# Three interleaved streams on one core: PSUM banks handed out in the order of the steps, and a new order of the steps

## The reference

```python
x = hidden                                                   # [4, 1024, 128]
x = layernorm(x + global_then_local_attention(x))            # 16 heads of 8, 4 key/value heads
x = layernorm(x + top2_of_8_experts(x))                      # 128 -> 512 -> 128, gelu
x = layernorm(x + linear_attention(x))                       # one head of 64, causal
for l in range(2):                                           # 8 heads of 64, windows of 64 tokens
    q, k, v = split(shift(x) @ wqkv[l])
    q, k = rotary(l2norm(q) * qs[l]), rotary(l2norm(k) * ks[l])
    x = x + local_attention(q, k, v) @ wo[l]
    h = layer_norm(shift(x)) @ w1[l] + b1[l]
    x = x + (a * gelu(g)) @ w2[l] + b2[l]                    # a, g = split(h)
x = layernorm(x_before_the_loop + x)
```

## Time and profile before

| | |
|---|---|
| median of three runs | 2167.21 us |
| the profiled execution, its own time | 2185.86 us |
| span of its records | 2184.1 us |
| mean granted TensorE clock | 0.861 of full |
| PE busy | 1683.2 us, 77% |
| PE weight loads | 1086.1 us, 50% |
| ACT busy | 1242.6 us, 57% |
| DVE busy | 1102.8 us, 50% |
| POOL busy | 778.1 us, 36% |
| mean DMA rate | 50 GB/s |

### The profile page before, as it was taken

How to read it: one execution, slowest core, us unless ns; L and a number is a source line. 1 busy time by engine, 2 the same in 40 slices (tenths; PEclk the granted TensorE clock), 3 DMA queues, 4 the chain that set the end, 5 groups by cost and what they waited for, 6 DMA issues and landing times.

```text
span 2184.1 us, 37425 instructions
## 1 busy us (share of the span) xinstructions
PE 1683.2 (77%) x13911; PEld 1086.1 (50%) x13911; DVE 1102.8 (50%) x2039; ACT 1242.6 (57%) x2819; POOL 778.1 (36%) x654
## 2 busy tenths in 40 slices
PE   4875477767559999869559999789689887778786
PEld 2124324434535765457334766467357555546454
DVE  4114601035586434584685334684863458475563
ACT  3663256843148989655147999553367565265462
POOL 2430161150159234720167233810471353062450
PEclk7787568976669999988779999978899999899898
DMA  4000023310121232100021233100223420010010
GB/s 144 1 1 1 0 78 98 112 41 1 46 77 48 76 95 89 46 8 1 20 80 45 76 92 93 46 9 1 63 69 90 127 75 23 5 45 21 25 28 10
DMA packets 64214, 109.52 MB, mean 50 GB/s; under 512 B 12464, under 2 KB 37284, under 8 KB 63908
## 3 DMA queue, kind: packets, MB, share of 16 engines
q1 hardware_dynamic: 58339, 98.23, 15.4%
q0 software_dynamic: 4096, 8.40, 1.3%
q10 hardware_dynamic: 1600, 0.52, 0.1%
HBM read 74.40 MB, written 15.93 MB: 41 GB/s over the span
## 4 chain that ended last, share of the span: by engine, by line
PE 42%; DVE 23%; ACT 14%; POOL 9%; issue 8%; DMA 2%; another core or an unknown queue 1%; SPq 1%; ACTq 0%; DVEq 0%; POOLq 0%
PE PH L826 5%; PE PD L1050 4%; PE PB L1151 3%; PE PB L1218 3%; ACT back_arena L1525 3%; POOL front_arena L2229 3%; PE PB L1238 3%; ACT front_arena L1360 2%; PE PD L874 2%; POOL fy L2297 2%; PE PB L1172 2%; ACT middle_arena L1473 2%; PE PD L1061 2%; PE PB L1274 2%; DVE back_arena L2085 2%
## 5 line engine op out<-in xcount | busy, mean ns | idle before, releaser
L1360 ACT ACTIVATE front_arena<-PD 128x1024 f32<-128x1024 f32 (+3 forms) x384 | 294.4, 815 | 96.5 <-PE PD L874 87.7
L2229 POOL TENSOR_TENSOR front_arena<-front_arena,tri 128x256 f32<-128x256 f32 x256 | 193.0, 771 | 338.5 <-ACT front_arena L1360 337.3
L2292 POOL TENSOR_TENSOR back_arena<-back_arena 128x512 f32<-128x512 f32 x128 | 182.7, 1434 | 270.2 <-DVE back_arena L2088 269.5
L1218 PE MATMUL PB<-wqkv,hT 128*128 128x512 f32 x384 | 226.7, 682 | 38.2 <-DVE back_arena L2088 13.3
L1525 ACT ACTIVATE back_arena<-PB,fnm 128x128 f32<-128x128 f32 x512 | 181.3, 373 | 85.8 <-DVE fnm L2095 85.5
L826 PE MATMUL PH<-front_arena 128*32 128x512 f32 (+3 forms) x1536 | 193.2, 575 | 37.5 <-POOL front_arena L2229 33.9
L2297 POOL TENSOR_TENSOR fy<-fm,minus_half 128x16 f32<-128x16 f32 x64 | 191.6, 2993 | 56.6 <-DVE fm L2111 54.7
L2282 POOL TENSOR_TENSOR bs_y<-bs_m,minus_half 128x4 f32<-128x4 f32 x24 | 24.3, 1011 | 400.0 <-DVE bs_m L2017 400.0
L2095 DVE TENSOR_REDUCE fnm<-PB 128x4 f32<-128x512 f32 x128 | 88.3, 690 | 153.3 <-PE PB L1238 135.6
L874 PE MATMUL PD<-front_arena 32*128 32x512 f16 (+3 forms) x768 | 128.9, 369 | 46.9 <-ACT middle_arena L1473 18.7
L1238 PE MATMUL PB<-back_arena 64*64 64x128 f32 x2048 | 145.0, 283 | 0.0
(11 more groups left out here) (294 smaller groups left out, 3553.9 us busy)
## 6 DMA issues: line engine op xcount, KB each, us to landing
W<-in_W SPq DMA_DIRECT2D x48, 514.0 KB
middle_arena<-in_W SPq DMA_DIRECT2D x44, 514.0 KB
back_arena<-back_arena SPq DMA_DIRECT2D x128, 128.0 KB
xpos<-x_tables SPq DMA_DIRECT2D x64, 128.0 KB
y_rows<-middle_arena SPq DMA_DIRECT2D x20, 256.0 KB, 5.4
middle_arena<-x_rows SPq DMA_DIRECT2D x8, 512.0 KB, 4.7
x_tables<-back_arena SPq DMA_DIRECT2D x1, 2048.0 KB, 7.5
out_y<-Nb SPq DMA_DIRECT2D x64, 32.0 KB, 1.6
```

Source lines behind the costliest of these rows:

```text
L1218: pe.matmul(p, hT[:, 128 * i:128 * i + 128], wqkv[:, l, c:c + 512], start=True, stop=True).then_inc(filled(b, "f" + n, l, i), 1)
L1360: act.activation(pb[:, :, 0:n], p[:, :, 0:n], ACT.Exp, scale=INV_SQRT_HD).then_inc(freed(b, "S", half, g, kc, jp), 1)
L2229: pool.tensor_tensor(pb, pb, tri[:, :].unsqueeze(1).to_broadcast([128, 2, 128]), ALU.mult).then_inc(sg("masked"), 1)
L2292: pool.tensor_tensor(T1[k % 2][:, hs, :], T1[k % 2][:, hs, :], T2[:, hs, :], ALU.add).then_inc(sg("rot"), 1)
```

## The change

Two things are changed together. First the places in PSUM: all eight banks are one tensor, a slot is (kind, first bank), and each step in turn is given that slot, of those it may use, whose banks were given out longest ago; it waits for the former users of all banks that the slot covers. Until the first step of a back, front and middle have three double slots (banks 0, 2 and 6) and the sums two single ones (4 and 5). From then on it is as before: double slots at 0 and 2, sums at 4, the back at 5, 6 and 7. Once the last global attention is done the back has bank 4 too, and after the last step that needs a double slot it has all eight.

Second, the table RUNS is another one. The number and kinds of the steps, what each does, and the order within each stream are the same.

```diff
 class Tickets:
-        self.size = {"D": 2, "H": 1, "B": 3}
-    def add(self, kind, *key):
-        k = self.next[kind] % self.size[kind]
+    def add(self, slots, *key):
+        def banks(slot):
+            return range(slot[1], slot[1] + (2 if slot[0] == "D" else 1))
+        def oldest(slot):
+            return max(self.stamp[k] for k in banks(slot))
+        slot = min(slots, key=oldest)
+        former = sorted({self.last[k] for k in banks(slot)} - {None})
...
+PAIRED = [("D", 0), ("D", 2)]
+SUMS = [("S", 4)]
+LATE = [("S", 5), ("S", 6), ("S", 7)]
...
-F153 M1 F4 M2 F6 M1 F2 M1 F2 M1 F2 M2 F1 M2 F4 M1 F2 M1 F4 M1 F4 M1 F4 M1
+F156 M2 F1 M1 F1 M2 F1 M4 F2 M1 F2 M1 F2 M1 F4 M5 F1 M1 F2 M1 F1 M2 F2 M3
...
+            if kind == "D":
+                t.add(PAIRED if begun else PAIRED + [("D", 6)], b, *(("gate",) if n == "gate" else label))
+            elif kind == "H":
+                t.add(SUMS if begun else SUMS + [("S", 5)], b, "O", rest[0], rest[1])
+            else:
+                slots = LATE + (SUMS if summed else []) + ([("S", k) for k in range(4)] if left["D"] == 0 else [])
...
         def fill(pe, *key):
-            kind, k, n = tk.at[key]
-            if n:
+            for (kind, k), n in tk.at[key][2]:
                 pe.wait_ge(sg(f"free_{kind}{k}"), n)
...
                     pe.wait_ge(sg("weights2"), 16 * len(second))
+                    fill(pe, "w_b1")
```

153 lines of the change are left out of this document (76 added, 77 removed).

## The result

The changed kernel takes 2067.58 us (median of 4 runs, 2057.81 to 2076.29), the kernel before 2165.92 in the same session (4 runs, 2161.36 to 2169.61). The ratio is 0.9546 with a 95% interval of 0.9497 to 0.9595: 98 us faster. I had predicted 2137 us, range 2100 to 2188.

What follows compares the result with a forecast made beforehand. No engine bounds the kernel; the order of the work does, by how well it fills PE. Terms 231 + 275 + 1077 + 300 + 271 = 2154 against a 2184 us span, 30 less, giving 2137 us, range 2100 to 2188.

Steps and rivals of the forecast that it cites:

- the fill: F1 with M0: the pieces of M0's chain sum to 275 us against 353, so B0 starts 78 us earlier.
- Experts under 115 us: Sign in F1 with M0: the prediction is wrong if M0's experts take over 115 us.
- Twelve pairs at 8.4 us: M0's experts within F1: twelve pairs take 100 us, against 126.3 before.
- the bound of 72: M0's experts: 72 us for twelve pairs if bound by the weights alone, with two pairs in flight.
- 933 us: From B0's start to M3's start: PE work of 933 us, which with 144 idle makes 1077.
- The sign that I had named for the opposite: Starts of F2 and F3: wrong if stretches with busy DVE and idle PE return with their full 27 us.
- the term of 300: M3 with the rest of B2: M3's chain pieces sum to 302, taken as 300 us, against 355 before.
- The chain bounds this stretch, not PE: M3 with the rest of B2: M3's dependent chain sets the time, with PE idle for 104 us.
- No PE row is in it, so in those tiles a free bank gains nothing: B3's tiles: the 10.29 us cycle has no PE row, so eight banks gain 3 us, bounds 0 and 24.
- Rival 1: B3, M3's stretch and F0: banks decide more, 43 us beyond the forecast, 2094 us; chance 0.20.
- Rival 2: M0 and M3: the experts' chain doesn't get shorter, price 74 us, 2211 us, or 2186 with two thirds; chance 0.13.
- Rival 3: Middle of the kernel: idle just moves, every round still loses 80 us, 1118 for 1077, 2178 us; chance 0.14.

Runs made afterwards that it cites:

- The loads in two parts: Changed kernel, with the first product's columns of each expert's weights loaded one product earlier, the rest as before: 2035.62 us, ratio 0.9377.
- without the early ones: Changed kernel without the third double slot (D6) and second sums bank (S5) ahead of the first back: 2102.0 us, ratio 0.9699.
- The late round alone: Kernel before with the new banks and old order through F3, M2, B1; then 92 steps of B2 alone, then M3 with B2's rest as changed: 2165.59 us.
- the second product first: Changed kernel, with the second product of expert pair i - 1 ahead of the first product of pair i: 2159.39 us, ratio 0.9946.
- thin weights: Changed kernel, but after the first four expert loads each fetches only 64 of 1028 columns: 2037.0 us, ratio 0.9400.
- the banks alone: Kernel before with the changed kernel's bank rule and the old table RUNS: 2150.91 us, ratio 0.9907.

## Why the prediction was wrong

By its terms, in us of the profiled span:

| stretch | predicted | measured | of which PE idle, predicted / measured |
|---|---|---|---|
| F0 | 231 | 231 | - / 90 |
| F1 with M0 | 275 | 275 | - / 80 |
| 506 to M3's start | 1077 | 1046 | 144 / 139 |
| M3 with the rest of B2 | 300 | 259 | 104 / 55 |
| B3 | 271 | 263 | - / 51 |
| sum | 2154 | 2074 | |

These are 80 us of span. The medians (2137 and 2067.6) differ by 69: I had carried the 18.65 us of the profiled execution of before over to the changed kernel, whose own was 8.7 us above its median. Three terms were wrong: M3 with the rest of B2 by 41 us, the middle by 31, B3 by 8.

**F0 and the fill** are right, the fill by errors that cancel. Its pieces: to the scatter 17 (25 predicted), scatter 23 (20), to the first product 8 (12), experts 125 (100), gather 24 with its lead (24), from there to B0's copy 77 (94). M0's experts and the path behind them are thus off by 25 and 17 us, in opposite directions; that the sum is 275 is luck. Experts under 115 us were one of my conditions, and it failed. The step that failed here is "Twelve pairs at 8.4 us", and the bound of 72 behind it, "two pairs in flight": the order of first and second product makes the loads come one after the other, at 10.4 us a pair. I had seen PE wait for up to 5 us and didn't follow the load back to the product that lets it start. The loads in two parts show what this was worth: 19 us up to the first back, 32 in all.

**The middle.** The idle per work is right: 139 / 907 is 0.153, I took 62 / 403 = 0.154. The step that failed is "933 us" of PE work, which was 907 (26 of the 31 us). I took the busy time of a round at its clock of 0.9 and carried it over. Busy time times clock is 933 x 0.895 = 835 predicted and 366.9 x 0.92 + 378.8 x 0.93 + 161.2 x 0.95 = 843 measured, the same work within 1%. So PE's time per product was lower at the higher clock. It belongs to the order and not to the banks: with the old banks the new order's middle has PE busy for 905.8 us, and 902.6 without the early ones. The shape came out as described: PE is busy for 906.9 of 1046 us (87%, forecast 85 to 88), and of the 24 slices of 45 us from 506 to 1586 none has it under 71%. The lowest, at the start of F3 with M2:

```profile
1091.00:1136.00 45.00, 32.27 (x194) 23.45 (x195) 39.29 (x91) 20.12 (x33) 23.66 (x20) 0.86 0.22 72
```

The sign that I had named for the opposite, PE idle for the full 27 us again at the starts of F2 and F3, didn't come: 11.7 us in the slice from 641, 12.7 in this one.

**M3 with the rest of B2** is the largest miss, 41 of 80 us. Its pieces, predicted and measured: to the scatter 25 / 16, scatter 22 / 35, then 12 / 10, experts 125 / 116, gather with its lead 27 / 23, to the last product of the linear attention 67 / 45, the end 24 / 15. I had taken most from M0 and M3 of the kernel before, where steps of the other streams stood between; those durations were what PE's order let them be, not the chain's own. So the step that failed is the term of 300, a sum of such pieces, and with it "The chain bounds this stretch, not PE": PE is busy for 204 of 259 us, and in the last 90 us for 63.2 (70%), where I had said under 55%:

```profile
1721.00:1811.00 90.00, 63.19 (x413) 44.89 (x412) 49.00 (x82) 30.73 (x64) 22.20 (x21) 0.84 0.09 26
```

The late round alone gives 262 us for this order behind the old middle, where my term of 300 should have held if the chain had that length of its own.

**The banks.** I took 3 us for F0 and 3 for B3, as terms of their own. B3 takes 263 us, 8 less than my 271 and 11 less than before (I had named 10 as the point from which I would be wrong), and 14 less than with the new order and three banks. And the early banks gave 27 us, not in F0, where I looked for them (231 us with and without them), but in the packed fill behind it. Costs read from the old order (7.0 us of such waits in F0) say nothing of the banks that a tighter order wants. The distance of 10.29 us per tile in B3 is still there. The rotary at the head of a tile, on the chain of the kernel after, and between two of them products of PE:

```profile
1833.76 0.69 DVE back_arena L2105
...
1836.70 1.04 PE PX L1257 x16
...
1844.06 0.69 DVE back_arena L2105
```

But the step built on it, "No PE row is in it, so in those tiles a free bank gains nothing", failed in two ways. In the changed kernel the profile's chain between two rotaries does go over PE (L1293 and L1257), at the same distance. And 10.29 us was read from one pair of tiles. POOL's power comes once for each tile; of its 14 distances in B3 before (seven in each layer) half are 10.3 to 10.4 us, but six are 12.3 to 16.0. Two tiles of the second layer, before and after:

```profile
2058.55 2.91 POOL L2297 TENSOR_TENSOR fy<-fm,minus_half 128x16 f32<-128x16 f32 x1 [0.29 <-DVE fm L2111]
2074.53 2.91 POOL L2297 TENSOR_TENSOR fy<-fm,minus_half 128x16 f32<-128x16 f32 x1 [0.28 <-DVE fm L2111]
```

```profile
1956.87 2.91 POOL L2317 TENSOR_TENSOR fy<-fm,minus_half 128x16 f32<-128x16 f32 x1 [0.28 <-DVE fm L2131]
1969.91 2.91 POOL L2317 TENSOR_TENSOR fy<-fm,minus_half 128x16 f32<-128x16 f32 x1 [0.28 <-DVE fm L2131]
```

These tiles came 16.0 us apart and now come 13.0. From the first power of this layer to its eighth it took 88.3 us (2033.07 to 2121.34) and now takes 81.3 (1932.89 to 2014.18): 7 of B3's 11 us. It is the fourth bank that gives them: the new order with three banks takes 88.2 us there, with four 81.3. The first layer's tiles gave nothing (73.5 and 73.7 us), the feed-forward parts the rest. Which wait made the long distances is not shown.

**The rivals.** Rival 1 (banks decide more, 2094) came nearest, but with the gains in the wrong places: B3 gave 11 us, a third of what it named, the early banks gave 27 in a stretch that it didn't name. Rival 2 (the experts' chain doesn't get shorter) was right in its mechanism for M0: its twelve pairs took 125 us, because the first product waited for weights. Its price fell with the rest: the first back began at 506 all the same, M3's experts took 116 us and not 140. Rival 3 (every round loses 80 us) is refuted by the middle's 139 us of idle in 1046. None had the clock in it.

The rule of the Trainium skill that the prediction weighed ("Perfetto Trace Analysis", section "Matmul Optimizations": use all eight PSUM banks) fits this case halfway. A fourth bank for the back shortens B3 from 276 to 260 us; with all eight it takes 263, which is no gain. Where the rule did pay was the fill, with 27 us.

What stays open: how much of the 25 us less of busy time is the change and how much the one execution that was profiled; which of D6 and S5 gives the early 27 us; and what set the long distances of B3's tiles.

## What to carry to other kernels

A duration in a merged order is not a price of the chain: before it is carried over, follow each wait back to the instruction that lets the load or the product start, and ask what bounds it once the work between is gone. Slots and order are one choice, not two terms: a tighter order needs its banks exactly where it is tight, and the old order's waits don't show it. When a wait is to be removed, look first at what the moved instruction would wait for; here the earlier load cost PE nothing, and the earlier product cost it new waits and a lower clock. And a distance read from one pair of tiles is not yet that of all tiles.

## What the runs showed of the hardware

Fewer stalls of PE and a higher granted clock came together. The mean granted clock of an execution was 0.849 to 0.865 in 36 runs of the kernel before and 0.878 to 0.888 in the four of the changed one, and no product was left out. In the experts of M1, M2 and M3 the second product first had 19, 12 and 8 us more idle and 15, 17 and 14 us more busy time, at a granted clock of 0.87, 0.83 and 0.86 instead of 0.97, that is a larger share of the time at 1.2 GHz. The Trainium skill ("TensorE: Matmul & The Clock Gate", section "What's actually happening") has the gate of this clock set by how busy PE has been recently; these rows agree in direction. The prediction had taken the clock as fixed by stretch.

Over a whole kernel it is a tendency and no price. The same 13911 products took 1683 us of PE busy time before, 1658 after the change, 1639 with the loads in two parts and 1628 with thin weights, where PE was idle for 501, 416, 402 and 398. But the late round alone had 1664 us busy at 500 idle, and the second product first 1696 at 467. Single executions differ as well: the same B3 with eight banks had PE busy for 204.4 us in the banks alone and 212.1 in the changed kernel.

On the chain above, the load of one expert tile's weights (514 KB) took 3.5 and 5.2 us. Loads of a sixteenth of the bytes still left waits of up to 2.7 us.
